# A decoder layer with linear attention: the quadratic part over 64 tokens instead of 128

## The chip, the cores and the metric

The kernel runs on one core of a Trainium2 chip. The metric is the device time of one execution, in microseconds (us). Five engines work side by side: TensorE (PE; its weight loads are listed as PEld), VectorE (DVE), ScalarE (ACT), GpSimd (POOL), and SyncE (SP), which issues most transfers. Each engine has a queue in order; semaphores tie them together.

## The reference

4 × 1024 tokens of width 256 pass through an attention layer without softmax (16 heads of width 16), a feed-forward network, two layer norms, and then a second network in which each token goes to one of eight experts. All is float32. The part that the change touches is the causal product at the end of the attention:

```python
qs = q * (sink_in / normal)[..., None]
vs = v * src_comp[..., None]
kv = jnp.cumsum(jnp.einsum('bhld,bhlm->bhldm', k, vs), axis=2)   # running sum of k v^T, per head
x = jnp.einsum('bhld,bhldm->bhlm', qs, kv) * sink_alloc[..., None]
attn = x @ Wo + bo
```

So a token's result is its query times the sum of k vᵀ over all tokens up to it. The kernel doesn't form that sum for each token. Within a chunk of tokens it multiplies all keys with all queries and masks what lies ahead (the quadratic part); what lies before the chunk enters by a state, the sum of k vᵀ up to there.

## The kernel before

The 4096 tokens are eight groups of 512; two groups make one sequence, so the second of each pair (`half == 1`) goes on from the state of the first. Each group runs through stages: `a` (projections of q, k, v, the running sums, the weights of conservation), `p` (the quadratic part, the output product, first layer norm), `h` and `b` (the feed-forward network, on the first and the second half of a group's tokens), `c` and `d` (second and third norms, the router, places of tokens). The group of stage `a` is one ahead of that of `p` and `h`, two ahead of `b`, three ahead of `c`, four ahead of `d` (`LAG`). For each engine a list written out in the source gives the order of the steps: `PE_FIRST`, `PE_ORDER`, `PE_LAST`, and the like for DVE, ACT, POOL. The middle list runs once for each period. `all_groups` (line 249) walks them. In the last period no `a` steps are left. Ahead of the periods come groups 0 and 1 with a list of their own; behind them comes the router's last work and then the tiles of the experts (`turn_rows`, `up`, `down` and their mixed forms), which the change doesn't touch.

The `p` stage before works on chunks of 128 tokens, four per group (`NC`). `share2` (line 747) spreads the weights, and VectorE's `scaled_q` (1571) writes the weighted queries `qs` and keys `kT`, heads along the partitions, tokens along the columns. Two heads of width 16 share 32 partitions. ScalarE's `split_q` (1094) makes two copies of the queries, with the odd or the even heads set to zero (`qm`). Then for each chunk:

- `turn_k` (781) turns the keys to tokens along the partitions, into bank `pm`; `take_k` (1103) copies them to `ktok`.
- `pairs` (756): for each 32 partitions, keys times both halves of `qm`: eight products of 256 columns into the four banks `BANK4`. VectorE's `mask` (1584) multiplies with a triangle, four times per chunk, into `sm`.
- `mix` (796): two full products of the state with the queries, then 16 of the masked pairs with the values `vpad`, all into `pm`; then eight that give the chunk's own sum of k vᵀ (into `ps0`). VectorE's `mix` (1597) adds it to `summed` and writes it with zeros between heads to `state` (lines 1603 and 1605); the next chunk's `mix` on TensorE waits for that.
- `take_x` (1108) copies the mixed values from `pm`, `attn_out` (826) multiplies with Wo, `first_sums` (1611) adds the residual.

The values come from `begin` (1486, line 1501): bias added, heads spread over `vpad`. The router's steps (`route`, `logit`, `count`) use bank `pm` too, and so `route` waits for `xatc`. The experts' weights use the room of the `p` stage's tiles, so SyncE loads them only when the last group's output product and state are done (592, 593). `unread_product` (697) is a product that nobody reads.

In float32 each product of the program, transposes aside, shows as two in the trace.

## Time and profile before

| | us |
|---|---|
| median of three executions | 822.36 (817.87 to 822.57) |
| the profiled execution | 819.06 |
| its span, first to last instruction | 817.3 |
| TensorE busy | 784.7 |
| VectorE busy | 572.2 |

The span begins with the first instruction of the program and ends with the last. An engine's busy time is the union of its instructions; a product's end on TensorE is modelled, so its busy time contains short waits. In a timeline, a row is a run of instructions of one kind: start, length, engine, line, what is written from what, the tile of the array (rows*columns), the moving operand, and the count. Line numbers are those of the kernel before.

### The profile page before, as it was taken

Reading aid. Unit: us, or ns where it says so; the run is one execution under the profiler, and the core shown is the slowest. Engines: PE = TensorE matmul, PEld = TensorE weight load, DVE = VectorE, ACT = ScalarE, POOL = GpSimd, SP = SyncE. Lnnn points to the kernel's source line nnn. Section 1 sums busy time; section 2 is a strip of 40 time slices with the busy share of each in tenths; the row PEclk is TensorE's granted clock in tenths of the full one; section 3 lists DMA queues with packets and bytes.
Section 4 is the critical chain, followed back from the end, with each engine's and each line's share of the span. In section 5 each row is a group of like instructions: output and inputs, shape, how many; then the busy total and the mean of one; then the engine's idle time right before and its main releaser. Section 6 shows DMA issues by size and latency. Waiting matters only on the chain.

```text
span 817.3 us, 18774 instructions
## 1 busy us (share of the span) xinstructions
PE 784.7 (96%) x6848; PEld 602.6 (74%) x6848; DVE 572.2 (70%) x1209; ACT 317.6 (39%) x586; POOL 338.4 (41%) x548
## 2 busy tenths in 40 slices
PE   8999999999999999999999989999999999999994
PEld 4476787687687677777777777788997778777762
DVE  7978768889899899899899894764663333433432
ACT  2332424433543543543444433343213444333442
POOL 8300402423434535525425444675334433334434
PEclk9989999999999999999999999999999999999998
DMA  8799997101000100100000101894569998888850
GB/s 279 231 331 325 321 313 237 52 1 48 6 15 16 51 8 21 53 8 21 28 7 9 41 7 32 303 360 159 188 195 398 373 343 323 308 315 296 292 194 13
DMA packets 75193, 133.22 MB, mean 163 GB/s; under 512 B 5725, under 2 KB 54111, under 8 KB 75104
## 3 DMA queue, kind: packets, MB, share of 16 engines
q1 hardware_dynamic: 71648, 123.05, 45.0%
q0 software_dynamic: 3168, 8.46, 2.8%
q8 instruction: 56, 0.92, 0.5%
q10 hardware_dynamic: 288, 0.52, 0.2%
q14 instruction: 33, 0.27, 0.1%
HBM read 89.35 MB, written 42.93 MB: 162 GB/s over the span
## 4 chain that ended last, share of the span: by engine, by line
PE 84%; DVE 6%; POOL 5%; issue 3%; ACT 1%; DMA 1%; POOLq 0%; ACTq 0%; DVEq 0%
PE bank L1000 11%; PE bank L965 10%; PE bank L852 7%; PE bank L884 6%; PE bank L895 6%; PE bank L864 5%; PE bank L656 5%; PE bank L814 4%; PE bank L776 4%; PE bank L1012 4%; PE bank L980 4%; PE bank L830 3%; PE bank L665 3%; PE bank L686 2%; PE bank L694 1%
## 5 line engine op out<-in xcount | busy, mean ns | idle before, releaser
L1321 POOL TENSOR_SCALAR vare<-mv 128x1 f32<-128x1 f32 x96 | 24.4, 254 | 255.7 <-DVE mv L1595 252.7
L965 PE MATMUL bank<-xsT,fc 128*128 128x128 f32 x800 | 94.4, 276 | 0.5 <-issue 0.5
L965 PEld LDWEIGHTS bank<-xsT,fc 128*128 128x128 f32 x800 | 91.4, 192 | 3.6 <-issue 3.4
L1588 DVE TENSOR_TENSOR sm<-bank,upto 128x512 f32<-128x512 f32 x128 | 79.3, 681 | 16.6 <-PE bank L776 16.5
L1000 PE MATMUL bank<-pj,act 128*128 x336 | 76.1, 379 | 0.8 <-DVE act L1783 0.8
L1180 ACT ACTIVATE relu<-bank 128x512 f32<-128x512 f32 x68 | 40.2, 595 | 91.4 <-PE bank L965 63.2
L852 PE MATMUL bank<-n1T,w1s 128*128 128x256 f32 x256 | 68.9, 392 | 2.6 <-ACT n1T L1124 1.8
L884 PE MATMUL bank<-n1T,w1s 128*128 128x256 f32 x256 | 69.3, 394 | 1.7 <-ACT n1T L1140 0.9
L1000 PEld LDWEIGHTS bank<-pj,act 128*128 128x128 f32 x336 | 62.2, 190 | 8.7 <-issue 1.1
L895 PE MATMUL bank<-w2s,hT 128*128 128x256 f32 x256 | 66.9, 385 | 0.0
L864 PE MATMUL bank<-w2s,hT 128*128 128x256 f32 x256 | 64.5, 380 | 0.0
L1324 POOL TENSOR_TENSOR rstd<-vare,minus_half 128x1 f32<-128x1 f32 x96 | 59.2, 617 | 8.0
L884 PEld LDWEIGHTS bank<-n1T,w1s 128*128 128x128 f32 x256 | 45.4, 192 | 16.2 <-ACT hT L1146 6.3
L1146 ACT ACTIVATE hT<-bank,b1s 128x256 f32<-128x256 f32 x64 | 30.1, 471 | 65.5 <-PE bank L884 65.5
L852 PEld LDWEIGHTS bank<-n1T,w1s 128*128 128x128 f32 x256 | 44.4, 189 | 14.9 <-issue 4.2
L1797 DVE COPY token<-xs 128x1 int32<-128x1 int32 x34 | 5.2, 153 | 70.4 <-PE bank L1000 47.4
L1380 POOL DMA_INDIRECT out_rows<-y,token x34 | 35.5, 1044 | 42.7 <-DVE y L1804 41.4
L864 PEld LDWEIGHTS bank<-w2s,hT 128*128 128x128 f32 x256 | 47.5, 190 | 6.7 <-issue 0.2
L656 PE MATMUL bank<-xT,wqkv 128*128 128x512 f32 x112 | 51.9, 608 | 0.0
L895 PEld LDWEIGHTS bank<-w2s,hT 128*128 128x128 f32 x256 | 47.4, 192 | 6.0
L1129 ACT ACTIVATE hT<-bank,b1s 128x256 f32<-128x256 f32 x64 | 30.3, 473 | 51.5 <-PE bank L852 51.5
L1374 POOL TENSOR_SCALAR mvare<-mmv 128x1 f32<-128x1 f32 x34 | 6.4, 189 | 101.8 <-DVE mmv L1802 101.6
(270 smaller groups left out, 1676.2 us busy)
## 6 DMA issues: line engine op xcount, KB each, us to landing
routed_rows<-empty SPq DMA_DIRECT2D x64, 520.0 KB, 8.6
fc<-in_fc SPq DMA_DIRECT2D x31, 1024.0 KB, 7.7
up_unit<-in_fc SPq DMA_DIRECT2D x24, 1024.0 KB, 8.6
pj<-in_pj SPq DMA_DIRECT2D x8, 1024.0 KB, 12.4
xrow<-in_fc SPq DMA_DIRECT2D x6, 1024.0 KB, 7.0
x<-in_x SPq DMA_DIRECT2D x8, 512.0 KB, 3.8
xT<-in_xT SPq DMA_DIRECT2D x7, 512.0 KB, 5.0
xs<-routed_rows SPq DMA_DIRECT2D x25, 130.0 KB, 5.4
```

Source lines behind the costliest of these rows:

```text
L656: last = nc.tensor.matmul(four[n][:], w[:, k, chunk(m)], xT[:, half, k, :], start=(k == 0), stop=(k == KT - 1))
L776: last = nc.tensor.matmul(BANK4[i][:, m * 2 * P:(m + 1) * 2 * P], kT[rows, half, m, chunk(c)], qm[rows, :, m, chunk(c)], start=True, stop= ...
L852: last = nc.tensor.matmul(pb[:, HALF], w1[:, k, chunk(f)], n1T[:, k, HALF], start=(k == 0), stop=(k == KT - 1), skip_group_check=True)
L864: last = nc.tensor.matmul(po0[:, c * D:c * D + D], hT[:, f % 2, chunk(c)], w2[:, f, :], start=(f == 0 and c == 0), stop=(f == FT - 1), ski ...
L884: last = nc.tensor.matmul(pb[:, REST], w1[:, k, chunk(f)], n1T[:, k, REST], start=(k == 0), stop=(k == KT - 1), skip_group_check=True)
L895: last = nc.tensor.matmul((po0, po1)[c // 2][:, (c % 2) * D:(c % 2) * D + D], hT[:, f % 2, chunk(c)], w2[:, f, :], start=(f == 0 and c % 2 ...
L965: last = nc.tensor.matmul(h_bank[n][:, chunk(f)], fc[:, at, k, chunk(4 * n + f)], xsT[:, k, :], start=(k == 0), stop=(k == KT - 1))
L1000: last = nc.tensor.matmul(to[:, 0:D], actT[j % 3][:, f, :], rows, start=(f == 0), stop=(f == FE - 1))
L1180: nc.scalar.activation(relu[:, n], src[:], ACT.Relu).then_inc(M["relu"].sem, 1)
L1324: nc.gpsimd.tensor_tensor(rstd[:, n, c], vare[:, n, c], minus_half[:], ALU.pow)\
L1380: nc.gpsimd.indirect_dma_start(out=out_d, out_offset=bass.IndirectOffsetOnAxis(ap=token[:, j % 3:j % 3 + 1], axis=0), in_=y[:, j % 3], in_ ...
L1588: nc.vector.tensor_tensor(sm[:, n], BANK4[n][:].rearrange("p (h t) -> p h t", h=4), upto[:].unsqueeze(1).broadcast_to([P, 4, P]), ALU.mult ...
```

## The change

Everything between `scaled_q` and `attn_out` is laid out for 64 tokens (`Q`) instead of 128, with the keys split instead of the queries. A masked pair block has 64 key tokens of even heads on the lower 64 partitions and the same 64 tokens of odd heads on the upper 64.

- `split_k` replaces `split_q`: ScalarE copies the keys, even and odd heads, to `km`. It now comes ahead of the transposes, which read `km`.
- `turn_k` makes four transposes per step into `ps1` and `pc` in turn, and all four steps come before the pairs; `take_k` copies 512 columns. `ktok` holds the whole group.
- `pairs` runs twice per group, for 256 tokens each: 32 products of 64 columns. `mask` runs 8 times per group instead of 16, on 512 columns as before.
- `update` is a step of its own (`p_upd`): the sums of all eight 64-token chunks, 64 products of 32 columns, into `ps0`. VectorE's `states` adds them up, eight additions in a chain; no spreading with zeros any more.
- `mix` runs twice per group: 32 products of a 32×32 state tile with 64 query columns, then 32 of the masked pairs, all into `ps1`. `take_x` copies 512 columns at once, `attn_out` makes both chunks of 128.
- `begin` writes the values with eight additions on 64 partitions per group instead of four on 128.
- `route` no longer waits for `xatc`. All order lists are written anew; the sizes of two spare tiles change.

The diff, cut to its core (most order lists, the setup of masks and renamed counts are left out; of removed lines none stands here, as the functions before are printed above):

```diff
+ND, Q = NC // 2, P // 2
...
 PE_FIRST = [
...
+    ("p_share2", 0, 0), ("e_proj", 2, 2), ("t_fill", 0, 2), ("p_kt", 0, 0), ("p_kt", 0, 1), ("p_kt", 0, 2),
+    ("p_kt", 0, 3), ("p_pairs", 0, 0), ("e_proj", 2, 3), ("p_upd", 0, 0), ("t_fill", 0, 0), ("p_mix", 0, 0),
+    ("a_dots1", 1, 0), ("p_out", 0, 0), ("t_shift", 0, 0), ("a_share1", 1, 0), ("t_fill", 0, 1), ("h_turn", 0, 0),
...
 PE_ORDER = [
+    ("p_share2", 0), ("b_turn", 0), ("a_proj", 0), ("a_proj", 1), ("b_turn", 1), ("a_proj", 2), ("a_proj", 3),
+    ("b_up", 0), ("a_proj", 4), ("a_proj", 5), ("d_count", 0), ("b_up", 1), ("b_down", 0), ("p_kt", 0), ("p_kt", 1),
+    ("b_down", 1), ("p_kt", 2), ("p_kt", 3), ("b_up", 2), ("c_route", 0), ("p_pairs", 0), ("b_up", 3),
+    ("b_down", 2), ("p_upd", 0), ("b_up", 4), ("b_down", 3), ("a_dots1", 0), ("p_mix", 0), ("b_up", 5),
+    ("p_out", 0), ("b_down", 4), ("b_up", 6), ("b_down", 5), ("b_up", 7), ("c_route", 1), ("a_share1", 0),
+    ("h_turn", 0), ("b_down", 6), ("h_turn", 1), ("b_down", 7), ("h_up", 0), ("p_pairs", 2), ("h_up", 1),
+    ("h_down", 0), ("c_route", 2), ("h_up", 2), ("p_mix", 2), ("h_down", 1), ("h_up", 3), ("c_route", 3),
+    ("h_down", 2), ("h_up", 4), ("a_dots2", 0), ("c_logit", 0), ("p_out", 2), ("h_down", 3), ("h_up", 5),
+    ("c_back", 0), ("a_comp", 0), ("h_down", 4), ("h_up", 6), ("h_down", 5), ("h_up", 7), ("h_down", 6),
+    ("h_down", 7),
 ]
...
 DVE_ORDER = [
+    ("p_share2", 0), ("c_sum2", 0), ("a_proj", 0), ("c_sum3", 0), ("a_proj", 1), ("a_proj", 2), ("c_sum2", 1),
+    ("a_proj", 3), ("a_proj", 4), ("a_proj", 5), ("a_prod", 0), ("d_count", 0), ("p_mask", 0), ("p_mask", 1),
+    ("c_sum2", 2), ("p_mask", 2), ("p_mask", 3), ("p_state", 0), ("c_sum3", 1), ("c_sum2", 3), ("c_sum3", 2),
+    ("a_dots1", 0), ("p_sums", 0), ("p_sums", 1), ("b_half", 0), ("c_sum3", 3), ("a_share1", 0), ("a_scan2", 0),
+    ("p_mask", 4), ("p_mask", 5), ("p_mask", 6), ("p_mask", 7), ("a_scan2", 1), ("a_dots2", 0), ("p_sums", 2),
+    ("p_sums", 3), ("a_comp", 0), ("b_add", 0), ("c_choose", 0),
 ]
...
 ACT_ORDER = [
+    ("a_proj", 0), ("b_turn", 0), ("b_turn", 1), ("a_proj", 1), ("a_proj", 2), ("a_proj", 3), ("b_up", 0),
+    ("p_share2", 0), ("b_up", 1), ("c_row", 0), ("p_pairs", 0), ("p_pairs", 1), ("p_pairs", 2), ("p_pairs", 3),
+    ("b_up", 2), ("b_up", 3), ("b_up", 4), ("c_route", 0), ("p_mix", 0), ("c_row", 1), ("b_up", 5), ("b_up", 6),
...
+        vpad = s1("vpad", [P, 2, 2 * NC, H // 2, 2 * DH])
+        km = s1("km", [P, KT, 2 * NC, 2, Q])
+        sm = s1("sm", [P, 4, 4 * P])
+        ktok = s1("ktok", [P, 2 * NC, D])
+        sums, carried = s1("sums", [P, 2 * NC, KT * 2 * DH]), s1("carried", [P, KT * 2 * DH])
...
+        def state_at(k):
+
+            return sums[:, k - 1] if k else carried[:]
+
+        def pair_columns(k, m):
+
+            at = (k % 4 // 2 * KT + m) * P + k % 2 * Q
+            return slice(at, at + Q)
...
+            def pairs(g, half, i):
+                d = i // 2
+                if d == 0:
+                    for e in range(2):
+                        ev[f"km{e}"].wait(pe, g, KT)
+                    ev["qp"].wait(pe, g, KT)
+                    ev["ktc"].wait(pe, g, NC)
+                else:
+                    ev["rden"].wait_if_any(pe, g + 1, 1)
+                    ev["scaled"].wait_if_any(pe, g + 1, 4)
+                ev["r1"].wait(pe, g, 2 * d)
+                ev["sm"].wait(pe, g, 4 * d)
+                for k in range(4 * d, 4 * d + 4):
+                    for m in range(KT):
+                        for j in range(4):
+                            rows = slice(32 * j, 32 * j + 32)
+                            last = nc.tensor.matmul(BANK4[j][:, pair_columns(k, m)],
+                                                    km[rows, m, k].rearrange("p e t -> p (e t)"),
+                                                    qs[rows, m, Q * k:Q * k + Q], start=True, stop=True,
+                                                    skip_group_check=True)
+                            if (k % 4, m) == (3, KT - 1):
+                                last.then_inc(S["s"], 1)
+
+            def turn_k(g, half, c):
                 if c == 0:
+                    for e in range(2):
+                        ev[f"km{e}"].wait(pe, g, KT)
+                    ev["qp"].wait(pe, g, KT)
                     if g == 0:
                         pe.wait_ge(masks_done, ALL_MASKS)
+                        ev["v"].wait(pe, 1, 8)
+                    ev["sig"].wait_if_any(pe, g + 1, 4)
+                    ev["v"].wait_if_any(pe, g + 1, 8)
+                elif c >= 2:
+                    ev["ktc"].wait(pe, g, c - 1)
+                for n in range(2):
+                    for m in range(KT):
+                        last = nc.tensor.transpose((ps1, pc)[c % 2][:, chunk(n * KT + m)],
+                                                   km[:, m, 2 * c + n].rearrange("p e t -> p (e t)"), ident[:])
                 last.then_inc(S["kt"], 1)
 
+            def update(g, half, _):
+
+                ev["ktc"].wait(pe, g, NC)
+                ev["v"].wait(pe, g, 8)
+                ev["sm"].wait(pe, g, 1)
+                for k in range(2 * NC):
+                    for m in range(KT):
+                        for j in range(HPT // 2):
+                            at = m * P + 32 * j
+                            to = (k * KT + m) * 32
+                            last = nc.tensor.matmul(ps0[32 * j:32 * j + 32, to:to + 32], ktok[:, k, at:at + 32],
+                                                    vpad[:, half, k, 4 * m + j, :], start=True, stop=True,
+                                                    skip_group_check=True)
+                last.then_inc(S["upd"], 1)
+
+            def mix(g, half, i):
+                d = i // 2
+                if g == 0 and d == 0:
                     pe.wait_ge(tables_in, 16 * 8)
+                ev["st"].wait(pe, g, 2 * NC)
+                ev["sm"].wait(pe, g, 4 * d + 2)
+                begun = set()
+                for k in range(4 * d, 4 * d + 4):
+                    if half == 0 and k == 0:
+                        continue
                     for m in range(KT):
+                        for j in range(HPT // 2):
+                            rows = slice(32 * j, 32 * j + 32)
+                            nc.tensor.matmul(ps1[rows, pair_columns(k, m)], state_at(k)[rows, 32 * m:32 * m + 32],
+                                             qs[rows, m, Q * k:Q * k + Q], start=j not in begun, stop=False,
+                                             skip_group_check=True)
+                            begun.add(j)
+                for k in range(4 * d, 4 * d + 4):
+                    for m in range(KT):
+                        for j in range(HPT // 2):
+                            if (k, m) == (4 * d, 0):
+                                ev["sm"].wait(pe, g, 4 * d + j + 1)
+                            last = nc.tensor.matmul(ps1[32 * j:32 * j + 32, pair_columns(k, m)],
+                                                    vpad[:, half, k, 4 * m + j, :], sm[:, j, pair_columns(k, m)],
+                                                    start=False, stop=False, skip_group_check=True)
                 last.then_inc(S["av"], 1)
+
+            def attn_out(g, half, i):
+                d = i // 2
+                ev["xatc"].wait(pe, g, d + 1)
+                ev["sm"].wait(pe, g, 4 * d + 3)
+                for c in range(2):
+                    for m in range(KT):
+                        last = nc.tensor.matmul(pa[:, c * D:c * D + D], xat[:, c, m, :], wo[:, m, :],
+                                                start=(m == 0), stop=(m == KT - 1), skip_group_check=True)
+                last.then_inc(S["wo"], 2)
...
             def route(g, half, c):
 
                 ev["xr"].wait(pe, g, c + 1)
+                if c == 0:
                     ev["acc"].wait(pe, g - 1, 1)
...
+            def split_k(g, half, _):
                 for m in range(KT):
+                    ev["kp"].wait(act, g, m + 1)
+                    ev["s"].wait(act, g - 1, 4 * ND)
+                    for e in range(2):
+                        nc.scalar.activation(km[:, m, :, e], kT[:, half, m].rearrange("p (k t) -> p k t", t=Q), ACT.Copy,
+                                             scale=parity[:, e:e + 1]).then_inc(S[f"km{e}"], 1)
 
             def take_k(g, half, c):
                 ev["kt"].wait(act, g, c + 1)
+                ev["upd"].wait(act, g - 1, 1)
+                nc.scalar.activation(ktok[:, 2 * c:2 * c + 2].rearrange("p n d -> p (n d)"), (ps1, pc)[c % 2][:], ACT.Copy)\
+                    .then_inc(S["ktc"], 1)
+
+            def take_x(g, half, i):
+                d = i // 2
+                ev["av"].wait(act, g, d + 1)
+                ev["wo"].wait(act, g, 2 * d)
+                nc.scalar.activation(xat[:].rearrange("p c m t -> p (c m t)"), ps1[:], ACT.Copy)\
+                    .then_inc(S["xatc"], 1)
 
...
+                ev["av"].wait(dve, g - 2, ND)
                 ev["proj"].wait(dve, g, 5 + n)
                 src = project_to(g)[1][n][:].rearrange("p (c j e d) -> p c j e d", c=2, e=2, d=DH)
+                dst = vpad[:, half].rearrange("p (c k) j w -> p c k j w", k=2)
+                for part in range(2):
+                    tokens = slice(Q * part, Q * part + Q)
+                    for e in range(2):
+                        nc.vector.tensor_tensor(
+                            dst[Q * e:Q * e + Q, 2 * n:2 * n + 2, part, :, DH * e:DH * e + DH], src[tokens, :, :, e],
+                            bv[tokens].rearrange("p (j e d) -> p j e d", e=2, d=DH)[:, :, e].unsqueeze(1)
+                            .broadcast_to([Q, 2, H // 2, DH]), ALU.add).then_inc(S["v"], 1)
...
+                nc.vector.tensor_tensor(sm[:, n].rearrange("p (h t) -> p h t", t=Q), BANK4[n][:].rearrange("p (h t) -> p h t", t=Q),
+                                        upto[:].unsqueeze(1).broadcast_to([P, 8, Q]), ALU.mult).then_inc(S["sm"], 1)
...
+            def states(g, half, _):
+                ev["upd"].wait(dve, g, 1)
+                for k in range(2 * NC - half):
+                    new = ps0[:, k * KT * 32:(k + 1) * KT * 32]
+                    into = sums[:, k] if k < 2 * NC - 1 else carried[:]
+                    ev["st"].wait(dve, g, k)
+                    if k or half:
+                        last = nc.vector.tensor_tensor(into, new, state_at(k), ALU.add)
+                    else:
+                        last = nc.vector.tensor_copy(into, new)
+                    last.then_inc(S["st"], 2 if half and k == 2 * NC - 2 else 1)
 
             def first_sums(g, half, c):
                 ev["xb"].wait(dve, g, 1)
                 ev["wo"].wait(dve, g, c + 1)
                 ev["n1"].wait(dve, g - 1, c + 1)
+                nc.vector.tensor_tensor(r1[:, c], pa[:, c % 2 * D:c % 2 * D + D], xb[:, c], ALU.add)\
```

## Rows read from the trace of the kernel before

**Rows 1.** The page, parts 1 and 2: busy time of each engine; DVE's slices; TensorE's clock by slice.

```profile
PE 784.7 (96%) x6848; PEld 602.6 (74%) x6848; DVE 572.2 (70%) x1209; ACT 317.6 (39%) x586; POOL 338.4 (41%) x548
DVE  7978768889899899899899894764663333433432
PEclk9989999999999999999999999999999999999998
```

**Rows 2.** Windows, one steady stretch: length, busy us of PE, PEld, DVE, ACT, POOL; clock.

```profile
300.00:355.00 55.00, 54.61 (x487) 41.13 (x479) 49.25 (x96) 25.10 (x50) 29.21 (x46) 1.00 0.09 30
```

**Rows 3.** Timeline of PE, one later chunk; columns: start us, length us, then the group.

```profile
201.69 0.38 PE L911 MATMUL bank<-ident,xrow 128*128 128x128 f32 x2
202.02 1.15 PE L776 MATMUL bank<-qm,kT 32*128 32x256 f32 x16
203.10 0.44 PE L793 MATMUL bank<-ident,kT 128*128 128x128 f32 x2
...
205.10 0.67 PE L806 MATMUL bank<-qs,state 128*128 128x128 f32 x4
205.71 1.13 PE L814 MATMUL bank<-sm,vpad 128*32 128x128 f32 x32
206.60 0.36 PE L822 MATMUL bank<-vpad,ktok 128*32 128x32 f32 x16
206.89 0.38 PE L740 MATMUL bank<-total_ex,earlier 128*128 128x1 f32 x2
```

**Rows 4.** Timeline of PE, one period from `share2` to `share2`.

```profile
278.18 1.14 PE L694 MATMUL bank<-spread,of_head 32*128 32x512 f32 x8
...
292.81 1.03 PE L895 MATMUL bank<-w2s,hT 128*128 128x256 f32 x4
294.07 1.15 PE L776 MATMUL bank<-qm,kT 32*128 32x256 f32 x16 [0.23 <-issue]
...
296.12 1.03 PE L895 MATMUL bank<-w2s,hT 128*128 128x256 f32 x4
296.98 1.03 PE L884 MATMUL bank<-n1T,w1s 128*128 128x256 f32 x4
...
341.65 1.14 PE L694 MATMUL bank<-spread,of_head 32*128 32x512 f32 x8
```

**Rows 5.** Timeline of PE, long runs of one kind late in the kernel.

```profile
541.96 3.74 PE L965 MATMUL bank<-xsT,fc 128*128 128x128 f32 x32
...
801.74 1.04 PE L991 MATMUL bank<-ident,relu 128*128 128x128 f32 x8
```

**Rows 6.** TensorE, group of line 822: count, busy us, mean ns of one, idle before.

```profile
L822 PE MATMUL bank<-vpad,ktok 128*32 128x32 f32 x512 | 13.4, 197 | 0.0
```

**Rows 7.** VectorE, groups by line: count, busy us, mean ns of one, idle before.

```profile
L1588 DVE TENSOR_TENSOR sm<-bank,upto 128x512 f32<-128x512 f32 x128 | 79.3, 681 | 16.6 <-PE bank L776 16.5
L1501 DVE TENSOR_TENSOR vpad<-bank,bvs 128x256 f32<-128x256 f32 x32 | 11.3, 407 | 0.5 <-PE bank L665 0.5
L1605 DVE TENSOR_TENSOR state<-summed,same_head 128x256 f32<-128x256 f32 x32 | 13.8, 433 | 1.1
L1603 DVE TENSOR_TENSOR summed<-summed,bank 128x64 f32<-128x64 f32 x28 | 6.0, 213 | 13.8 <-PE bank L822 13.7
```

**Rows 8.** ScalarE, groups by line: count, busy us, mean ns of one, idle before.

```profile
L1098 ACT ACTIVATE qm<-qs,parity 128x512 f32<-128x512 f32 x16 | 11.4, 710 | 1.1 <-DVE qs L1575 1.1
L1106 ACT ACTIVATE ktok<-bank 128x256 f32<-128x256 f32 x32 | 12.0, 376 | 14.7 <-PE bank L793 14.6
L1196 ACT ACTIVATE act<-bank 128x512 f32<-128x512 f32 x4 | 2.2, 594 | 2.9 <-PE bank L991 2.9
```

**Rows 9.** Timeline of PE in the period without projections.

```profile
474.44 0.64 PE L793 MATMUL bank<-ident,kT 128*128 128x128 f32 x2 [1.26 <-DVE acc L1691]
...
478.18 1.15 PE L776 MATMUL bank<-qm,kT 32*128 32x256 f32 x16
```

**Rows 10.** Timeline of PE, the first pair products.

```profile
44.81 1.15 PE L776 MATMUL bank<-qm,kT 32*128 32x256 f32 x16 [0.52 <-issue]
```

306 lines of the change are left out of this document (88 added, 218 removed), and 7 rows, old and new, of tables (DVE_LAST, POOL_LAST).

## The prediction

> **What bounds the kernel now.** I read the page first: TensorE is busy 96% of the span, VectorE 70%, and VectorE's busy digits lie at 8 and 9 from the eighth to the twenty-third slice, that is, in the periods of the eight groups, and at 3 and 4 later [rows 1]. So the late half is TensorE's alone and the change doesn't touch it; in the first two thirds two engines are near full. The windows view makes that sharper: of 55 us TensorE is busy 54.61 and VectorE 49.25 [rows 2]. Busy time on TensorE is modelled to each product's end, so it hides short stalls. I therefore went to the timeline and read start to start: four products of 256 columns take 0.86 us when nothing disturbs them (296.12 to 296.98), but the same four take 1.26 us (292.81 to 294.07) when the next line must wait [rows 4]. A period, from one `share2` to the next, is 341.65 − 278.18 = 63.47 us [rows 4], and nearly all of it is TensorE streaming. What is saved counts accordingly: a microsecond saved on TensorE in a period is a microsecond of the kernel; one saved on VectorE counts only where TensorE waits for it.
>
> **What the quadratic part costs TensorE before, per group.** Prices come from start to start in one chunk [rows 3]; every program product of float32 appears as two products (line 776: 8 in the program, 16 in the row). Pairs: 203.10 − 202.02 = 1.08 us. One transpose: eight of them span 1.04 us and two span 0.38 us, so each more costs 0.66/6 = 0.11 us [rows 3, 5]. The two transposes before the pairs start at 201.69 and should stream until 201.91; the pairs start at 202.02, so changing to another shape of the array costs 0.11 us. I charge it once to each block of pairs and of mix. Mix with the update of the sums: 206.89 − 205.10 = 1.79 us, of which the part with the state (line 806) is 0.61, the masked part (line 814) 0.89 and the update (line 822) 0.29. Transposes of the keys: 0.27 for two. A group has four chunks: pairs 4 × 1.19 = 4.76, mix and update 4 × 1.90 = 7.60, less about 0.3 because the first chunk of every other group has no state product, transposes 4 × 0.27 = 1.08. Sum 13.1 us of the 63.47.
>
> **The same after.** *Pairs*: 64 program products, 128 in the trace, each loading 128 weight columns for only 64 moving columns. A stream of products with 128 weight columns and 128 moving columns shows a start each (3.74 − 0.27)/31 = 0.112 us [rows 5], so a weight load costs at most that. Four row tiles run side by side: line 776 does four products of 256 columns in (1.08 − 0.21)/4 = 0.22 us, about the 0.216 that one such product takes alone in line 895 [rows 3, 4]; 0.21 is what the block lasts beyond its four rounds. I take one round of four per 0.112: a block of 16 rounds is 1.79 + 0.11 + 0.21 = 2.11, two blocks 4.2. From below, half the columns at the old rate are 128 × 0.216/16 + 2 × 0.32 = 2.4 for both; from above, no faster than line 776 per product (0.067 × 128) would be 8.6. I take 4.2 because the limit is a weight load, and that row is the only one with an equal load.
>
> *Masked part*: 128 products of 64 columns where there were 128 of 128. Line 814 takes 0.89/32 = 0.028 us each; halved 0.014, 64 of them 0.9 us per block (from above, if a short product costs what a long one did, 1.8). *State part*: two full 128×128 products per chunk become, for each 64 tokens, eight on 32 rows and 32 columns; 128 in the trace per group (112 in even groups). The trace has no such tile. From below they overlap four deep, as row tiles in line 776 and column tiles in line 814 do: 0.014 each; from above they run one after another: 0.054 each (a quarter of 0.216). I take 0.014, because both kinds of tile that the trace does have overlap so. A mix block is then entry 0.11, state 0.9, change of shape 0.17 (line 806's 0.61 less 4 × 0.11), masked part 0.9, exit 0.13 = 2.2; two are 4.4, 4.35 on the mean.
>
> *Update*: now one step of 128 products of 32 columns instead of four steps of 16. Line 822's sixteen span 0.36 us and one lasts 0.197 [rows 3, 6], so they start 0.16/15 = 0.011 us apart: 128 × 0.011 + 0.11 + 0.13 = 1.65. From above, with the block's ends in the price, 0.018 each: 2.5.
> Here a rule of the skill speaks against the change: the Trainium skill, "TensorE: Matmul & The Clock Gate", section "Wait — 56ns, not 53.3ns?", says that starts never come closer than about 25 ns, however few the columns. By it the update alone would be some 3.4 us a group. The trace disagrees for column tiles taken in turn, 11 ns, and the measurement decides.
>
> *Transposes of the keys*: 16 per group, as both masked halves are turned, in blocks of four: 16 × 0.11 + 4 × 0.05 = 1.96. *Output product* (line 830): same count.
> Sum after: 4.2 + 4.35 + 1.65 + 1.96 = 12.2. Gain 0.95 us per group, 7.6 over eight groups.
>
> **VectorE, per group.** Eight masks fewer: −8 × 0.681 = −5.45. Values: eight additions of 256 elements on 64 partitions instead of four on 128. Rows with half the partitions and the same elements are not among those I rest on, so I bound: at least half the time (0.2), at most the whole 0.407; taken whole, +1.63. State: four pairs of 0.213 and 0.433 become eight of 0.213 in one chain, −0.88 [rows 7]. Net −4.7 us, from 49.25 to about 45 in 55. What TensorE gets of it lies between 0 and 4.7 a period. The wait before line 776 was 0.40, of it 0.11 the change of shape [rows 3, 4]; I take 0.8, somewhat under three such waits of 0.29, since TensorE is already 99% busy there [rows 2]; over seven periods 5.6. The new chain of eight additions stands between update and mix, about 8 × 0.213 = 1.7 us; the planned order puts `b_up` 4, `b_down` 3 (0.86 each) and `a_dots1` between them, which covers it. If that cover is gone, mix waits up to 1.7 us in a period.
>
> **ScalarE, per group.** The four split copies stay (0.71 each), on keys now. Four copies of keys grow from 256 to 512 columns, 4 × (0.594 − 0.376) = +0.9; four copies of mixed values of 256 columns become two of 512, 2 × 0.594 − 4 × 0.376 = −0.3 [rows 8]. ScalarE is busy 25 of 55 us [rows 2], so the work is hidden. Its place is not: transposes, and after them pairs, now wait for the split. In a steady period the projections, the first products of `b_up` and the count stand ahead of the transposes on TensorE and cover it; behind the split in ScalarE's queue stands `b_up` 1, whose activation TensorE needs next, as before. In the first group and in the period without projections nothing covers it (second rival). I add nothing for these two, because there the serial rounds of pairs, mask, mix and output fall from four to two at the same time.
> No transfer is added. The expert loads wait for the last group's state and output, both earlier in their period now.
>
> **Sum.** The profiled execution took 819.06 us (span 817.3 and 1.8 around it), 0.4% under the median of 822.36. 819.06 − 7.6 − 5.6 = 805.9: I predict 806.
>
> **Rivals.**
> *Small products don't overlap (slower).* The state products of four row tiles write one bank. If they go one after another, 960 of them pay 0.040 more: +38, so about 844. For it: no row shows such a tile. Against: their partitions differ, as do line 814's. It decides from 13.2/960 = 0.014 us extra each, where the whole gain is gone. Chance 0.12; it includes the pairs or the masked part at their upper prices, which end on the same side (+35 and +14).
> Beside this: the Trainium skill, "PSUM — Partial Sum Buffer", section "PSUM bank collisions raise a hardware error", quotes that different row tiles can't access one PSUM bank at the same time, but lets different quadrants of a bank be used together; the new products are each on a quadrant of their own. No row of the kernel before shows which holds for speed.
> *A floor under each start (slower).* If no product could start within 0.025 us of the last, the update would pay 0.014 more on each of 1024 products, masked and state part 0.011 on each of 1984: +36, about 842. For it: no run of more than sixteen such short products stands in the rows. Against: those sixteen start 0.011 apart [rows 3, 6]. Chance 0.04. (It is the rule named at the update.)
> *Later starts eat the gain (no change).* The first pairs start at 44.81 [rows 10]. After the change they come behind four blocks of transposes and four copies of 0.594, some 3 to 4 us later; the same in the period without projections, where TensorE already waits 1.26 us at 474.44 and pairs start at 478.18 [rows 9]. With 7 us lost there and nothing from VectorE: 819 − 7.6 + 7 = 818. For it: those stretches are chains. Against: two rounds fewer. Chance 0.22.
> *VectorE was the hidden bound (larger gain).* If half of the 4.7 us reaches TensorE, 2 us × 7 = 14, and the two chain stretches give 4 together: 819 − 7.6 − 18 = 793. For it: VectorE at 90% [rows 2]. Against: TensorE's own streams leave little room in 63.47. Chance 0.17.
> My forecast, 798 to 812 as its own range, has 0.45.
>
> **How the numbers follow.** Low end: the larger gain, 792. High end: no change, 818, with the update at its upper price (0.007 × 128 × 8 = 7.2), about 826; beyond lies the rival whose products don't overlap. A measurement of this kernel can tell about 1% from no change, so the line is at 811 against 819. Faster by over 1%: 0.60 (the forecast, but for its upper edge, and the larger gain); within 1%: 0.24; slower: 0.16.
>
> **What would show it.** Right: pairs blocks of 64 products near 2.1 us, mix blocks near 2.2, an update near 1.6, a period near 61.7 us, VectorE near 45 of 55. Wrong: state products 0.05 us apart; mix idle until a VectorE addition; TensorE idle before the key transposes in the first group; a lower granted clock around 45 us for longer than now (the page shows 8 tenths in one slice there [rows 1]).

## The result, and the profile after

| | before | after |
|---|---|---|
| median of seven runs, us | 819.34 (817.83 to 822.91) | 828.88 (825.55 to 835.57) |
| span of the profiled execution, us | 817.3 | 827.2 |

The ratio is 1.0116, with a 95% interval of 1.0076 to 1.0156: the change makes the kernel 1.2% slower. Forecast was 806 us, and the range ended at 826.

The page of the kernel after, in the lines of [rows 1]:

```profile
PE 777.4 (94%) x8784; PEld 603.9 (73%) x8784; DVE 534.4 (65%) x1173; ACT 321.4 (39%) x570; POOL 357.4 (43%) x546
...
DVE  7984575887797797797798785455663333333332
...
PEclk9997899999999999999999999999999999999998
```

TensorE is busy 7.3 us less and VectorE 37.8 us less, as intended, and the span is 9.9 us longer. So the work shrank and the waits grew. Where they grew shows in the starts of `share2`, line 694 on TensorE's timeline (start us, length us). Second and eighth group, before:

```profile
93.76 1.14 PE L694 MATMUL bank<-spread,of_head 32*128 32x512 f32 x8
...
468.88 1.14 PE L694 MATMUL bank<-spread,of_head 32*128 32x512 f32 x8
```

After; the two rows in the middle bound the period that answers to [rows 4]:

```profile
108.53 1.14 PE L694 MATMUL bank<-spread,of_head 32*128 32x512 f32 x8
...
292.08 1.14 PE L694 MATMUL bank<-spread,of_head 32*128 32x512 f32 x8
...
355.54 0.71 PE L694 MATMUL bank<-spread,of_head 32*128 32x512 f32 x4
...
481.21 1.14 PE L694 MATMUL bank<-spread,of_head 32*128 32x512 f32 x8
```

| stretch | before | after | difference | forecast |
|---|---|---|---|---|
| start to `share2` of the second group | 93.76 | 108.53 | +14.8 | 0 |
| six periods | 375.12 | 372.68 | −2.4 | −10.5 |
| from there to the end of the span | 348.4 | 346.0 | −2.4 | −2.7 |

(The forecast column shares out its 13.2 us: 0.95 on TensorE and 0.8 from VectorE in each of six periods, the rest behind them.) There are two questions: why does the start lose 14.8 us, and why do the periods gain so little? The one of [rows 4] took 63.47 us and takes 63.46.

TensorE in the start after the change:

```profile
42.78 1.14 PE L694 MATMUL bank<-spread,of_head 32*128 32x512 f32 x8 [0.87 <-DVE spread L1536]
...
48.16 1.22 PE L699 MATMUL bank<-ones_t,ident 128*128 128x256 f32 x2 [2.33 <-DVE vpad L1521]
49.18 3.26 PE L792 MATMUL bank<-ident,km 128*128 128x128 f32 x16
53.21 2.02 PE L771 MATMUL bank<-qs,km 32*128 32x64 f32 x64 [0.78 <-ACT ktok L1118]
...
57.07 1.00 PE L806 MATMUL bank<-vpad,ktok 128*32 128x32 f32 x93
59.66 0.51 PE L806 MATMUL bank<-vpad,ktok 128*32 128x32 f32 x35 [1.59 <-issue]
...
62.35 1.50 PE L824 MATMUL bank<-qs,sums 32*32 32x64 f32 x48 [1.56 <-issue]
63.78 1.49 PE L833 MATMUL bank<-sm,vpad 128*32 128x64 f32 x43
68.66 0.75 PE L833 MATMUL bank<-sm,vpad 128*32 128x64 f32 x19 [3.39 <-issue]
```

VectorE's last state sum in the same stretch:

```profile
62.02 0.22 DVE L1625 TENSOR_TENSOR carried<-bank,sums 128x64 f32<-128x64 f32 x1
```

Two things are new. The first pairs (line 771) come at 53.21 instead of 44.81 [rows 10], 8.4 us later, behind sixteen transposes in a row; 2.6 us of it stand already at `share2` of the first group (42.78, before 40.16). And three times TensorE stands still in or before a block of short products, and the view names no releaser ("issue"), 6.5 us together. Twice, for 5.0 us, a block is cut in its middle. The third time, before the state products (line 824), it is a wait after all: they need all eight state sums, and the last ends at 62.24, 0.11 us ahead of them. In all ten variants below they start 0.10 to 0.11 us behind that sum, too.

In the six periods the waits view for 108.5 to 481.2 us names two waits on VectorE (total us, times, longest); no line of the kernel before waits for more than 1.5 us in total in its six periods:

```profile
PE bank L656 <- DVE qs L1596: 4.0, 5, 0.9
PE bank L792 <- DVE vpad L1521: 3.0, 2, 2.5
```

Line 656 is the next projection, which waits for the scaled queries. Line 792 is the key transposes, which write a bank that still holds the next group's projected values until VectorE's value additions (line 1521) have read them.

### The profile page after: what moved, and what is told of

The parts are those of the page before. It is cut to its first block, busy times and chain, and to the rows that moved or that the text cites. A ratio compares the mean times of both kernels' runs of the same rounds, so it can differ in the third digit from the quotient of the medians.

```text
span 827.2 us, 22408 instructions
## 1 busy us (share of the span) xinstructions
PE 777.4 (94%) x8784; PEld 603.9 (73%) x8784; DVE 534.4 (65%) x1173; ACT 321.4 (39%) x570; POOL 357.4 (43%) x546
## 4 chain that ended last, share of the span: by engine, by line
PE 64%; DVE 17%; POOL 8%; issue 8%; ACT 1%; POOLq 0%; DVEq 0%; ACTq 0%
PE bank L978 10%; PE bank L1013 10%; PE bank L866 5%; PE bank L1025 4%; PE bank L993 4%; PE bank L771 4%; PE bank L878 3%; PE bank L656 3%; POOL rstd L1341 3%; PE bank L909 3%; PE bank L898 2%; PE bank L844 2%; DVE cc L1489 2%; PE bank L792 2%; PE bank L665 2%
## 5 line engine op out<-in xcount | busy, mean ns | idle before, releaser
L1338 POOL TENSOR_SCALAR vare<-mv 128x1 f32<-128x1 f32 x96 | 32.4, 338 | 255.0 <-DVE mv L1616 250.6
L1341 POOL TENSOR_TENSOR rstd<-vare,minus_half 128x1 f32<-128x1 f32 x96 | 64.9, 676 | 8.1 <-POOL vare L1338 0.2
L1609 DVE TENSOR_TENSOR sm<-bank,upto 128x512 f32<-128x512 f32 x64 | 40.5, 683 | 30.6 <-PE bank L771 30.5
L866 PEld LDWEIGHTS bank<-n1T,w1s 128*128 128x128 f32 x256 | 47.5, 194 | 8.5 <-ACT hT L1144 1.5
L898 PEld LDWEIGHTS bank<-n1T,w1s 128*128 128x128 f32 x256 | 45.1, 190 | 10.8 <-issue 2.4
L1385 POOL DMA_INDIRECT routed_rows<-xrow,slot x32 | 36.1, 1130 | 31.2 <-DVE slot L1715 17.4
```

What stands on the lines that cost most here:

```text
L866: last = nc.tensor.matmul(pb[:, HALF], w1[:, k, chunk(f)], n1T[:, k, HALF], start=(k == 0), stop=(k == KT - 1), skip_group_check=True)
L898: last = nc.tensor.matmul(pb[:, REST], w1[:, k, chunk(f)], n1T[:, k, REST], start=(k == 0), stop=(k == KT - 1), skip_group_check=True)
L1341: nc.gpsimd.tensor_tensor(rstd[:, n, c], vare[:, n, c], minus_half[:], ALU.pow)\
L1385: nc.gpsimd.indirect_dma_start(out=xs_d, out_offset=bass.IndirectOffsetOnAxis(ap=slot[:, half, c:c + 1], axis=0), in_=xrow[:, half, c, :], ...
L1609: nc.vector.tensor_tensor(sm[:, n].rearrange("p (h t) -> p h t", t=Q), BANK4[n][:].rearrange("p (h t) -> p h t", t=Q), upto[:].unsqueeze(1 ...
```

## The experiments

All are edits of the changed kernel unless said; the times are medians of at least four executions and the ratios go against the kernel before on the same chip.

**The clearing transfers moved.** From 26 us on, SyncE sends 64 transfers of 520 KB that clear the routed rows; they keep the 16 DMA engines full until about 140 us. In this run they wait:

```diff
             load_xT(2, 0)
-            for g in range(G):
+            load_xT(3, 1)
+            ev["qp"].wait(sp, 1, KT)
+            for g in range(GPG):
                 empty_tiles(g)
+            load_xT(4, 0)
+            load_x(2)
+            for g in range(GPG, G):
+                empty_tiles(g)
...
```

> The changed kernel with one edit on SyncE's queue: the 64 transfers that clear the routed rows (520 KB each, issued from 25.9 us on, the 16 DMA engines full to about 125 us) wait until the second group's scaled queries are made (about 110 us); the loads of later inputs are issued ahead of them. Nothing is left out. Theory 'instructions arrive late': the TensorE idle times of 1.59, 1.56 and 3.39 us that end with no releaser inside the first group's state, mixing and masked products (59.7, 62.4, 68.7 us) come from instruction fetches (1.0 to 1.2 us each) that compete with these transfers. Then they vanish, the first product of share2 of the second group comes at about 102 us instead of 108.5, and the same idle times turn up in the blocks of the second and third group, which now run under the transfers; the time falls by 3 to 8 us where the later groups lose less than the first, and stays near 829 where they lose as much. Rival 'the products themselves': the blocks wait for something of their own (banks, order), so the idle times of 6.5 us stay in the first group, share2 of the second group stays at 108 us and the time at 827 to 830.

841.01 us (838.91 to 842.35), ratio 1.0267 [1.0243, 1.0290]. TensorE's timeline, with the start free of transfers and the periods under them:

```profile
57.08 1.30 PE L813 MATMUL bank<-vpad,ktok 128*32 128x32 f32 x128
...
63.51 1.75 PE L840 MATMUL bank<-sm,vpad 128*32 128x64 f32 x64
...
128.64 0.67 PE L813 MATMUL bank<-vpad,ktok 128*32 128x32 f32 x53 [2.16 <-issue]
...
135.66 0.64 PE L831 MATMUL bank<-qs,sums 32*32 32x64 f32 x30 [1.12 <-issue]
...
200.62 0.42 PE L693 MATMUL bank<-cc,head_at 128*32 128x128 f32 x7 [2.93 <-issue]
...
225.79 0.27 PE L840 MATMUL bank<-sm,vpad 128*32 128x64 f32 x1 [2.73 <-issue]
```

The same 128 and 64 products now run whole in the first group, and blocks that had run nearly without a break are cut where the transfers went. `share2` of the second group comes at 104.6, 4.0 us earlier (6.5 were expected, but the state products at 62.07 still wait for VectorE's sums, which end only 0.27 us earlier). The two periods behind it take 137.5 us instead of 121.0. The idle times follow the transfers. That the time could rise by 12 us I had not expected; 10.3 us of these two periods are such idle times, against 1.4 in the changed kernel, and the granted clock is 0.95 in them. How the other 7.6 of the 16.5 us lost come about was not followed up.

> The kernel before with the same edit on SyncE's queue (the 64 clearing transfers wait for the second group's scaled queries). It shows no idle time without a releaser above 0.6 us between 18 and 110 us. Theory 'instructions arrive late': its blocks are half as dense, the fetches keep up, so the time stays within 2 us of 819. Rival 'the transfers slow everything in the start': it gains as much as the changed kernel does, 3 us or more.

The kernel before with the same edit: 818.76 us (817.98 to 825.35), ratio 1.0002 [0.9983, 1.0020]. Its longer products don't suffer, whether the transfers lie in the start or in the periods.

**Half of the first group's value additions.**

```diff
-                    for e in range(2):
+                    for e in range(1 if g == 0 else 2):
...
-.then_inc(S["v"], 1)
+.then_inc(S["v"], 2 if g == 0 else 1)
```

> The changed kernel with half of the first group's eight value additions left out (the four of the odd heads, so that these values stay zero; the other four count twice on the semaphore). VectorE's stretch ahead of the first share1 shrinks by 4 x 0.45 = 1.8 us. Theory 'the late start of the first group is carried through': the first product of share1 comes at 23.3 us instead of 25.1, and share2 of the first group, the first pairs and the whole rest come 1.8 us earlier: about 827. Rival 'it is swallowed by the chain behind it' (normalisation, splits, transposes and their copies set the first pairs): the first pairs at 53.2 us move by less than 0.5 us and the time stays at 828 to 829.

826.07 us (824.36 to 830.81), ratio 1.0089 [1.0063, 1.0115]. `share1` came at 24.48 us, only 0.6 earlier, as the projection ahead of it ran at a low clock (0.60 from 21 to 25 us, after TensorE had been busy 1.09 of the 4 us before); the first pairs came at 51.72, 1.5 earlier; but idle times of 2.00 and 3.81 us in the middle of blocks put `share1` of the second group at 77.2, later than in the changed kernel (76.8). The interval overlaps that of the changed kernel, so this run decides nothing on the total.

**The counts put back.**

```diff
 PE_ORDER
-    ("p_share2", 0), ("b_turn", 0), ("a_proj", 0), ...
+    ("p_share2", 0), ("b_turn", 0), ("d_count", 0), ("a_proj", 0), ...
 DVE_ORDER
-    ..., ("a_proj", 1), ("a_proj", 2), ..., ("a_prod", 0), ("d_count", 0), ("p_mask", 0), ...
+    ..., ("a_proj", 1), ("d_count", 0), ("a_proj", 2), ..., ("a_prod", 0), ("p_mask", 0), ...
```

> The changed kernel with the routing counts put back to where the kernel before has them: on TensorE between share2 and the first projection, on VectorE after the second value step. Theory 'the periods gave their gain to a wait': the 0.9 us for which the first projection waits for the scaled queries in five periods is filled by work that is to be done anyway, the period shrinks from 63.4 us per two groups by about 1.6, and the time falls by 3 to 5 us, to about 825. Rival 'another wait takes its place' (the half turn on the normalised tokens, share2 on the shares): the wait of the projection goes and another grows by as much; the period and the time stay within 1 us.

828.12 us (827.85 to 829.97), ratio 1.0117 [1.0095, 1.0138]: no change. The rival held, at a place I had not named. The waits view for the six periods:

```profile
PE bank L792 <- DVE vpad L1521: 7.4, 6, 2.5
...
PE bank L656 <- DVE qs L1596: 0.6, 1, 0.6
```

The projection's wait went from 4.0 to 0.6 and the transposes' from 3.0 to 7.4. Both wait for one row of work on VectorE behind `share2`: queries, keys, query scans, eight value additions.

`share2` of the second and eighth group:

```profile
106.39 1.14 PE L694 MATMUL bank<-spread,of_head 32*128 32x512 f32 x8
...
481.94 1.14 PE L694 MATMUL bank<-spread,of_head 32*128 32x512 f32 x8
```

The six periods take 375.6 us, 2.9 more than in the changed kernel. The start takes 2.1 less, although the edit doesn't touch it: here the update runs whole, and the masked products are cut for only 0.37 us. So the start of one profiled execution can't be compared with that of another to better than 2 us.

**The transposes taken off that row.** With the counts back, the transposed keys go to the routing bank (`pm`) instead:

```diff
-                    ev["v"].wait_if_any(pe, g + 1, 8)
+                    ev["acc"].wait_if_any(pe, g - 3, 1)
...
-nc.tensor.transpose((ps1, pc)[c % 2][:, chunk(n * KT + m)],
+nc.tensor.transpose((ps1 if g == 0 else pm, pc)[c % 2][:, chunk(n * KT + m)],
```

(The pairs take over the wait for the values, the routing transposes wait for the key copies.)

> The changed kernel with the counts put back (as in the run before, which made no difference) and the transposed keys of all groups but the first written to the routing bank instead of a bank from which VectorE still reads the next group's projected values, so that the key transposes no longer wait for the eight value additions (the pairs do). Theory 'VectorE's value additions are now what TensorE waits for after share2': the waits of the projection (4.0 us in all) and of the key transposes (3.0 us, 7.4 us with the counts back) both go, six periods take 366 to 369 us instead of 372.7, time 822 to 825. Rival 'VectorE's whole row of work sets the period': the wait turns up at the pairs or at the products after them, time 827 to 830.

822.08 us (818.62 to 824.02), ratio 1.0020 [1.0001, 1.0038], 6.8 us below the changed kernel. `share2` of the second and eighth group:

```profile
106.69 1.14 PE L694 MATMUL bank<-spread,of_head 32*128 32x512 f32 x8
...
473.23 1.14 PE L694 MATMUL bank<-spread,of_head 32*128 32x512 f32 x8
```

Six periods take 366.5 us instead of 372.7, and 9.0 less than in the run before, from which this one differs in the bank alone (6.0 us by the medians of the whole time). In their waits view the transposes' wait is gone, the projection's is 0.6 us, and no new wait above 1.4 us stands in their place. So VectorE's row was not the period's length; the bank that the transposes shared with the values was in the way.

**The clears in four parts**, of 16 transfers each: at once, and after the mixed values of the first, second and third group.

```diff
-            for g in range(G):
+            for g in range(2):
                 empty_tiles(g)
+            load_xT(3, 1)
+            ev["av"].wait(sp, 0, ND)
+            for g in range(2, 4):
+                empty_tiles(g)
...
```

> The changed kernel with the 64 clearing transfers issued in four parts of 16 (about 23 us each): at once, and after the mixed values of the first, second and third group, stretches in which TensorE runs mostly long products. Nothing is left out. Theory 'instructions arrive late while the transfers run': the idle times without a releaser, 6.5 us in the first group of the changed kernel and about 10 us in the second and third group of the kernel with the late transfers, both go; share2 of the second group comes at about 104 us, and the periods stay at 57.9, 63.2 and 62.5 us; time 822 to 825. Rival 'any delay of the transfers only moves the loss': idle time without a releaser of 5 us or more in the blocks of a later group, time 828 or more.

823.39 us (822.40 to 824.76), ratio 1.0040 [1.0016, 1.0065], 5.5 us below the changed kernel. `share2` of the second group comes at 103.86, against 108.53 in the changed kernel and 106.39 with the counts put back. The timeline shows no block of the start cut in its middle; the idle time of 1.54 us before the state products ends 0.10 us behind VectorE's last state sum. TensorE's mean granted clock from 17 to 105 us is 0.84 here, 0.86 in the changed kernel and 0.96 in the kernel before (windows view): the lower clock of the start is real, but this gain came without any rise of it.

**Keys before queries in the first group** (the two loops of the scaling swapped for `g == 0`).

> The changed kernel, in its first group the two products that scale the keys ahead of the two that scale the queries on VectorE, so that ScalarE's split of the keys begins 1.2 us earlier. Theory 'the serial line split, transposes, copies, pairs sets the first group': key transposes, pairs and share1 of the second group come 1.2 us earlier (52.0 and 75.6 us), time about 827.5. Rival 'the wait for the next group's value additions sets it' (the fill and the transposes wait for it until 48.2 us): less than 0.5 us, time 828 to 829.

830.41 us (827.52 to 830.93), ratio 1.0119 [1.0095, 1.0143]. The rival held: the transposes start at 48.81, 0.4 us earlier, because TensorE's queue has the fill ahead of them, which waits for the second group's values until 48.27.

**The three edits together.**

> The changed kernel with the three edits together: transfers in four parts, counts back with the transposed keys in the routing bank, and the first group's keys ahead of its queries; nothing is left out. Theory 'three separate losses': the gains add up, 5 + 5 + 1 us off 829, so about 818, level with the kernel before or 1 to 2 us below it. Rival 'VectorE's row sets the period': only the gain of the transfers is left, 823 to 825.

815.96 us (812.95 to 819.74), ratio 0.9947 [0.9926, 0.9967], 12.9 us below the changed kernel, where 6.8 and 5.5 were measured singly: two separate losses that add up.

**Pairs first in the first group.**

```diff
 PE_FIRST
-    ("t_fill", 0, 2), ("p_kt", 0, 0), ... ("p_kt", 0, 3), ("p_pairs", 0, 0), ("e_proj", 2, 3)
+    ("p_pairs", 0, 0), ("t_fill", 0, 2), ("p_kt", 0, 0), ... ("p_kt", 0, 3), ("e_proj", 2, 3)
```

> The joined kernel (816.0 us), in its first group the pair products ahead of the key transposes, which now go to two banks that the pairs do not use; VectorE takes the four masks and the state sums ahead of the second group's query scans and tables. Nothing is left out. Theory 'what is left of the late start is the line split, transposes, copies, pairs, which the kernel before does not have in a row': the first pairs come at about 47.5 to 48.5 us instead of 53.2 (44.8 in the kernel before), the state update at about 53.5 instead of 57.1, share1 of the second group at 68 to 69.5 us instead of 72.1, and the time falls by 2.5 to 4 us, to 812 to 813.5. Rival 'VectorE's row in the start sets share1 of the second group': the pairs come earlier and share1 of the second group stays at 72 us, time 815 to 817.

817.20 us (815.64 to 818.03), ratio 0.9958 [0.9943, 0.9973]: not faster than the joined kernel. The cut shows TensorE's list alone; VectorE's order in the first group and the banks of the key transposes change with it. The pairs did come at 47.41, but the update (line 821) behind them did not follow:

```profile
47.41 2.01 PE L786 MATMUL bank<-qs,km 32*128 32x64 f32 x64 [1.57 <-ACT km L1128]
...
55.01 3.78 PE L690 MATMUL bank<-xT,wqkv 128*128 128x512 f32 x4 [2.69 <-ACT x L1111]
58.72 1.94 PE L821 MATMUL bank<-vpad,ktok 128*32 128x32 f32 x128
```

It stood in TensorE's queue behind an early projection that waits for ScalarE. One more exchange sets it free:

```diff
-    ("p_kt", 0, 3), ("e_proj", 2, 3), ("p_upd", 0, 0), ...
+    ("p_kt", 0, 3), ("p_upd", 0, 0), ("e_proj", 2, 3), ...
```

> The kernel with the pairs first (817.2 us), and on TensorE in the first group the state update ahead of the last of the third group's early projections, behind which it waited for 2.7 us and then ran from 58.7 us, at half clock; VectorE stood idle for 6.3 us until it came. Theory 'the start is set by the line up to the state sums': the update comes at 53 to 54 us, VectorE's idle time falls below 2 us, share1 of the second group comes at 68 to 70 us instead of 73.2 and the time falls by 3 to 5 us, to 812 to 814. Rival 'VectorE's row in the start, or a lower clock, sets share1 of the second group': it stays at 72 us or later, time 815 to 818.

812.41 us (809.05 to 813.75), ratio 0.9910 [0.9890, 0.9931]. This version beats both kernels, 0.9% below the one before.

```profile
54.45 1.05 PE L821 MATMUL bank<-vpad,ktok 128*32 128x32 f32 x98 [0.69 <-ACT ktok L1134]
...
62.10 0.48 PE L848 MATMUL bank<-sm,vpad 128*32 128x64 f32 x19 [1.64 <-issue]
...
69.16 1.14 PE L707 MATMUL bank<-spread,of_head 32*128 32x512 f32 x8 [0.26 <-issue]
...
100.89 1.14 PE L707 MATMUL bank<-spread,of_head 32*128 32x512 f32 x8
...
465.90 1.14 PE L707 MATMUL bank<-spread,of_head 32*128 32x512 f32 x8
```

Its six periods take 365.0 us, 10.1 less than before the change. Its start is still 7.1 us later than before (100.89 against 93.76). Of these, 2.9 stand at `share2` of the first group (43.03 against 40.16), 1.5 come up to `share1` of the second (69.16 against 64.74) and 2.7 between its `share1` and `share2` (31.73 us against 29.02). In that last stretch the granted clock is 0.84, and 1.00 in the kernel before (windows view); from 73 to 81 us it is 0.52, and a pairs block there takes 3.69 us instead of 2.01. How much of the 7.1 us the clock makes was not tried.

**Where the blocks break.** In the changed kernel and in four of its variants (half of the value additions, counts put back, transposes in the routing bank, keys first) the idle times cut the update after 93 of 128 products, if at all, and the masked products after 43 of 64. Eight unread products of one column are put ahead of the key transposes:

```diff
+                if _ == 2:
+                    for n in range(8):
+                        nc.tensor.matmul(po1[:, 0:1], ident[:], ones_t[:, 0:1], start=True, stop=True, ...)
```

> The changed kernel with eight unread products of one column (16 products in the trace) put on TensorE's queue behind the fill ahead of the first key transposes; they are work of their own, some 0.5 us. In the changed kernel and in three of its variants the idle times without a releaser split the first group's blocks at the same products: the update after 93 of 128, the masked products after 43 of 64. Theory 'TensorE has run out of instructions': the breaks are at fixed places of the instruction stream and move back by 16 products, so the update breaks after 77 (if its break is there at all) and the masked products after 27; time 827 to 832. Rival 'a bank, a semaphore or the products themselves': the breaks stay at 93 and 43.

829.64 us (827.99 to 830.17), ratio 1.0122 [1.0090, 1.0154].

```profile
63.19 1.30 PE L809 MATMUL bank<-vpad,ktok 128*32 128x32 f32 x128
...
67.46 0.88 PE L836 MATMUL bank<-sm,vpad 128*32 128x64 f32 x27
70.20 1.18 PE L836 MATMUL bank<-sm,vpad 128*32 128x64 f32 x35 [1.87 <-issue]
```

The masked products now break after 27, sixteen earlier, as expected; the update, which began 6 us later here, ran whole. The break belongs to a place in TensorE's stream of instructions, not to a product, a bank or a semaphore.

The pages before and after list a DMA queue for instructions (packets, MB, share of 16 engines):

```profile
q8 instruction: 56, 0.92, 0.5%
...
q8 instruction: 71, 1.16, 0.6%
```

The kept traces have the start and end of each of its packets, of 16 KB. Every idle time shown above that cuts a block ends 1.2 to 1.6 us after such a packet has ended. For the changed kernel's at 59.66 and 68.66 the packets run from 57.34 to 58.36 and from 66.18 to 67.33, for the shifted kernel's at 70.20 from 67.81 to 68.96. The idle time before the state products keeps no such distance (0.4 to 6.2 us over the variants). In the first 150 us packets last 0.9 to 1.5 us with the transfers and without. But the two that start at 57.34 and 66.18 under the transfers start at 54.76 and 59.09 where the transfers wait, though the blocks up to 57 us run at the same times in both kernels. So the blocks wait for instruction packets, and under the transfers these start late.

## Why the prediction was wrong, step by step

**TensorE's prices: right, and a little better than priced.** From the period of 292 to 356 us:

```profile
312.19 2.01 PE L771 MATMUL bank<-qs,km 32*128 32x64 f32 x64
314.13 1.13 PE L898 MATMUL bank<-n1T,w1s 128*128 128x256 f32 x4
...
316.05 1.30 PE L806 MATMUL bank<-vpad,ktok 128*32 128x32 f32 x128
317.28 1.13 PE L898 MATMUL bank<-n1T,w1s 128*128 128x256 f32 x4
...
320.21 0.87 PE L824 MATMUL bank<-qs,sums 32*32 32x64 f32 x48
321.02 1.10 PE L833 MATMUL bank<-sm,vpad 128*32 128x64 f32 x64
322.05 1.13 PE L898 MATMUL bank<-n1T,w1s 128*128 128x256 f32 x4
```

Start to start, a pairs block is 1.94 us (2.11 forecast), the update 1.23 (1.65; both forecasts contain 0.11 for the change of shape), the state part 0.81 for 48 products, 0.017 each (0.014), the masked part 1.03 (0.9). That a weight load limits the pairs, as assumed, no run shows. The state products of four row tiles overlap, so the first rival (0.054 each) falls. The Trainium skill, "PSUM — Partial Sum Buffer", section "PSUM bank collisions raise a hardware error", warns that different row tiles can't use one bank at the same time, and counts conflicts by quadrant of the bank; here four row tiles, each on its own quadrant of one bank, do overlap, at 0.017 us each.

The floor under each start falls too: 128 products in 1.23 us are 0.0096 us apart. The floor of about 25 ns in the Trainium skill, "TensorE: Matmul & The Clock Gate", section "Wait — 56ns, not 53.3ns?", does not hold for these tiles taken in turn.

**VectorE: the work right, its effect of the wrong sign.** It is busy 46.19 of 55 us (third of the busy times in this row of the windows view), 45 were forecast, against 49.25 [rows 2]:

```profile
314.00:369.00 55.00, 53.40 (x714) 40.70 (x711) 46.19 (x94) 23.98 (x46) 29.71 (x45) 1.00 0.10 31
```

The value additions took 420 ns each on 64 partitions (407 on 128 [rows 7]): half the partitions saved nothing, as assumed. The step that failed is "what TensorE gets of it lies between 0 and 4.7 a period". The lower end should have been negative: busy time fell, but the eight additions now stand in one row behind `share2`, and TensorE waits for their end before it may transpose keys. The change newly makes this wait, as it puts the transposed keys into a bank that still holds the values; the count that covered the first projection was moved as well. In place of 0.8 us gained per period, some 1.2 were lost (4.0 and 3.0 us over six).

The six periods in the windows view (length, TensorE's busy time): before, after, with the transposes in the routing bank, and in the last and fastest version:

```profile
93.76:468.88 375.12, 368.55 (x3396) 1.00 0.19 58
...
108.53:481.21 372.68, 361.32 (x4848) 1.00 0.16 48
...
106.69:473.23 366.54, 360.93 (x4849) 1.00 0.15 48
...
100.89:465.90 365.01, 360.36 (x4848) 1.00 0.26 80
```

TensorE's work shrank by 7.2 us, where 5.7 were forecast; its idle time should have shrunk by 4.8 and grew by 4.8, from 6.6 to 11.4 us. With the waits taken out the six periods gain 8.6 and 10.1 us, near the 10.5 forecast, but that is in part luck: TensorE's work is then 7.6 and 8.2 us less, and its idle time only 1.0 and 1.9 us less. By this view, which counts short stalls as work, VectorE's shorter work was worth a fifth to two fifths of its term. The period of [rows 4] comes to 62.8 us in both, not to 61.7; others gain up to 2.6 us.

**The first group: "I add nothing for these two" is the step that failed most.** I argued that fewer serial rounds pay for the split, the transposes and the copies. The first pairs come 8.4 us later, not 3 to 4. Of this, 2.6 us lie ahead of the chain: VectorE's value additions before the first `share1` take 3.58 us instead of 1.40, and the projection ahead of it runs at a granted clock of 0.64 instead of 1.00. The other 5.8 are the chain and the fill in its way. Behind the pairs the state sums hold up the mix, a wait that the prediction named for a mix without cover and priced at nothing here. The order experiment shows that the chain counts: once pairs and update were both freed, the time fell by 3.5 us (815.96 to 812.41; 3.0 by the ratios, as the chips differ); with the pairs alone it did not. The period without projections was judged with it and was no loss: from `share2` of the eighth group to the end the kernel is 2.4 us shorter.

**What no step contained: TensorE runs out of instructions.** The trace holds 8784 products instead of 6848 [rows 1], in dense blocks of 0.010 to 0.017 us each, and in the start they share the DMA engines with the clearing transfers. Spreading the transfers gave back 5.5 us. It is shown that the idle time follows the transfers, that its place moves with the instruction stream, and that it ends 1.2 to 1.6 us behind a packet of the instruction queue. Why a packet starts late under the transfers, in a queue or in the memory, is not seen in the trace.

**The rivals.** The nearest was "later starts eat the gain" (818 us, chance 0.22): the right place, at 3 to 4 us for the start, which lost 14.8, and without the other two causes. Of the signs named beforehand, three did show: the idle time ahead of the first key transposes (2.33 us at the fill), the mix idle until a VectorE addition (in the first group), and the lower clock. The clock is not what gave back 5.5 and 6.8 us, as these came at a mean clock of 0.84 and 0.83 in the start; its share in the 7.1 us that the start still loses is open. (Two slips in the sums changed nothing: half of 4.7 is 2.35 and not 2, and the larger gain is 793 in one place and 792 in the other.)

By medians: of the 16.5 us between 828.9 and 812.4, the bank of the transposes with the counts accounts for 6.8, the transfers for 5.5, the order in the first group for 3.5; 0.7 is left unassigned.

## What to carry to other kernels

An engine's busy time saved is not the bound of what a change can do: list, for each moved or split piece, which bank or buffer it now holds and who waits for it, and let the price of that wait be below zero. An order made for one set of instructions has to be looked at again where no steady state covers it, in the first group above all, and one freed step shows its gain only when the next one in the same queue is free as well. Splitting work into many short products also asks more of the instruction supply; look for idle time without a releaser in the middle of a block, and keep large transfers out of that stretch. Before an idle time is put down to that, look whether a producer ended just ahead of its end: one of the three here was such a wait.

## What the hardware showed unexpectedly

- Short products stream at 0.0096 us apart (column tiles, 32 columns) and 0.017 us apart (32×32 tiles, 64 columns) while instructions are there; such blocks stand still for up to 3.9 us at fixed places of the instruction stream, until 1.2 to 1.6 us after a 16 KB packet of the instruction queue has ended. Full DMA engines make it worse but are not all of it: in the last version 1.64 us are left (62.10, behind a packet from 59.74 to 60.70) with the DMA engines at a share of 0.00 from 59.74 to 62.10.
- The kernel before, whose blocks are half as dense, loses nothing under the same transfers (ratio 1.0002), wherever they lie.
- A VectorE addition of 256 elements takes as long on 64 partitions (420 ns) as on 128 (407 ns).
